# The last ticks of a fused cross-attention and DiT block written out call by call, with the MLP's copies, last normalisations and modulations on VectorE

## The reference

```
x = x + attention(q from ada_ln(x), k and v from ada_ln(ctx)) @ Wp            # layer CROSS0
x = x + gate_a * (attention(modulate(ln(x))) @ W_proj)                        # layer SELF1
x = x + attention(q from ln(x), k and v from ln(ctx)) @ W_cproj               # layer CROSS1
h = modulate(ln(x), shift_m, scale_m)                                         # 16 x 128 x 128
x = x + gate_m * (gelu(h @ W_mlp1 + b_mlp1) @ W_mlp2 + b_mlp2)                # inner width 512
```

## Time and profile before

| what | value |
|---|---|
| median of 3 runs | 291.34 us |
| the profiled execution's own time | 289.38 us |
| its span in the profile | 287.6 us |
| PE busy | 244.8 us, 85% |
| ACT busy | 219.7 us, 76% |
| DVE busy | 217.9 us, 76% |
| POOL busy | 135.8 us, 47% |
| granted PE clock, mean | 0.976 of full speed |

### The profile page before, as it was taken

The page is one execution under the profiler, slowest core; times in us unless marked ns, Lnnn a source line. Parts: engine busy times, 40 slices in busy tenths (PEclk is TensorE's granted clock), DMA queues, the critical chain, the costliest instruction groups (busy, mean ns, idle before and its releaser), DMA issues.

```text
span 287.6 us, 10124 instructions
## 1 busy us (share of the span) xinstructions
PE 244.8 (85%) x3811; PEld 171.0 (59%) x3811; DVE 217.9 (76%) x452; ACT 219.7 (76%) x399; POOL 135.8 (47%) x286
## 2 busy tenths in 40 slices
PE   1836888998898998989999899998998788887995
PEld 1523544766666666665666666676666455554865
DVE  6887886989789797887988899888997776313323
ACT  5327296897978879788798887988879688799940
POOL 8450723836336173363846738466275163420500
PEclk9975899999999999999999999999999999999999
DMA  6085965433446335452433424324244000000112
GB/s 202 10 189 145 254 139 169 134 97 100 128 131 147 101 98 132 128 132 61 109 98 82 114 56 119 98 71 115 60 113 109 10 5 6 3 2 0 36 53 59
DMA packets 34223, 27.44 MB, mean 95 GB/s; under 512 B 4904, under 2 KB 33920, under 8 KB 34176
## 3 DMA queue, kind: packets, MB, share of 16 engines
q1 hardware_dynamic: 32678, 25.54, 34.1%
q10 hardware_dynamic: 1498, 1.26, 1.9%
HBM read 6.46 MB, written 1.06 MB: 26 GB/s over the span
## 4 chain that ended last, share of the span: by engine, by line
PE 39%; ACT 23%; issue 12%; DVE 11%; POOL 9%; DMA 4%; SPq 1%; ACTq 1%; POOLq 0%; DVEq 0%
PE all_ps L469 8%; ACT probs L739 6%; PE all_ps L534 6%; ACT normed L705 6%; PE keyed_ps L520 5%; POOL parts L1117 4%; PE all_ps L576 4%; PE score_ps L495 4%; PE all_ps L565 3%; PE all_ps L557 3%; DVE rest L924 3%; DMA stack_k<-parts 3%; ACT parts L719 3%; DVE normed L909 2%; POOL parts L1115 2%
## 5 line engine op out<-in xcount | busy, mean ns | idle before, releaser
L932 DVE TENSOR_REDUCE neg_max<-score_ps 128x8 f32<-128x1024 f32 x96 | 117.3, 1222 | 18.8 <-PE score_ps L495 17.9
L739 ACT ACTIVATE probs<-keyed_ps 128x1024 f32<-128x1024 f32 x96 | 98.3, 1024 | 18.7 <-PE keyed_ps L520 14.5
L534 PE MATMUL all_ps<-probs,values 128*32 128x128 f32 x1536 | 54.4, 277 | 0.9 <-ACT probs L739 0.5
L534 PEld LDWEIGHTS all_ps<-probs,values 128*32 128x32 f32 x1536 | 37.9, 109 | 17.7 <-issue 8.9
L520 PE MATMUL keyed_ps<-stack_q,stack_k 64*128 64x128 bf16 x768 | 37.8, 217 | 6.0 <-ACT probs L739 5.6
L495 PE MATMUL score_ps<-stack_k,stack_q 62*128 62x128 bf16 x768 | 38.2, 219 | 5.5 <-DMA stack_k<-parts 1.9
L1102 POOL CAST max_parts<-neg_max 128x16 bf16<-128x16 f32 x48 | 9.8, 204 | 64.3 <-DVE neg_max L932 64.3
L495 PEld LDWEIGHTS score_ps<-stack_k,stack_q 62*128 62x128 bf16 x768 | 23.9, 95 | 16.1 <-issue 10.8
L520 PEld LDWEIGHTS keyed_ps<-stack_q,stack_k 64*128 64x128 bf16 x768 | 23.6, 94 | 16.4 <-ACT probs L739 13.8
L1085 POOL TENSOR_TENSOR rstd<-var_eps,minus_half 128x4 f32<-128x4 f32 x24 | 24.4, 1016 | 18.2 <-DVE var_eps L897 18.0
L469 PE MATMUL all_ps<-normed_t,w_qk 128*128 128x512 f32 x48 | 28.8, 694 | 0.0
(11 more groups left out here) (104 smaller groups left out, 402.1 us busy)
## 6 DMA issues: line engine op xcount, KB each, us to landing
stack_q<-parts SPq DMA_DIRECT2D x72, 128.0 KB, 2.5
stack_k<-parts SPq DMA_DIRECT2D x66, 128.0 KB, 2.8
gate<-gate_d SPq DMA_DIRECT2D x16, 128.0 KB, 3.2
stack_q<-max_rows SPq DMA_DIRECT2D x96, 4.0 KB
xs<-in_x_dram SPq DMA_DIRECT2D x4, 256.0 KB, 3.3
cs<-in_ctx_dram SPq DMA_DIRECT2D x4, 256.0 KB, 4.1
out_dram<-xs SPq DMA_DIRECT2D x8, 128.0 KB, 1.8
stack_k<-parts ACTq DMA_DIRECT2D x6, 128.0 KB, 3.6
```

Source lines behind the costliest of these rows:

```text
L534: mm = pe.matmul(ps[QUAD * a:QUAD * (a + 1), c * T:(c + 1) * T], values[:, u // PER % STACKS, u % PER * PAIRS + CP * c + a, 2 * e:2 * e + ...
L739: act.activation(probs[:, n % 3, :], keyed_ps[:, :, :].rearrange("t e n -> t (e n)"), ACT.Exp, scale=float(D) ** -0.5).then_inc(probs_read ...
L932: dve.tensor_reduce(neg_max[:, u % 2, :, CP * c:CP * (c + 1)], score_ps[:, :, :].rearrange("t e (a k) -> t e a k", k=T), AX.X, ALU.max, ne ...
```

## The change

The loops of all engines end at tick 44 (`DRAIN`), and from there each engine has a written list of calls; `DRAIN_USES` repeats PE's list for the ring. On ACT `leave_hidden` is gone for pieces 0 to 11, on DVE it is new; pieces 12 to 15 stay on ACT with their Gelu. Groups 14 and 15 are normalised by DVE's `normalise` and modulated by a new `modulate_mlp` on DVE, where ACT did both; POOL leaves out the two offset instructions for them. `activate_hidden` now waits for one piece at a time. Pieces 0 and 1 still have their ticks 41 and 42. The diff, cut to its core:

```diff
-        LAST = 57
-        UP_AT = (41, 42, 44, 44, 44, 45, 46, 46, 48, 48, 49, 50, 51, 52, 52, 53)
-        DOWN_AT = (49, 50, 51, 51, 53, 54, 55, 56)
-        GELU_AT = (48, 49, 51)
-        ADD_AT = (50, 52, 52, 52, 53, 53, 53, 54)
+        UP_AT = (41, 42)
+        DVE_FROM = 14
+        DRAIN = 44
         ACT_NORMS = (0,)
...
+        DRAIN_USES = [("max", 46), ("proj", 42), ("out", 43), ("up", 2), ("up", 3), ("turn", 43),
...
+        USES = HEAD_USES + [use for tick in range(FIRST, DRAIN) for use in at_tick(tick)] + DRAIN_USES
...
+            move_max(46)
+            move_max(47)
...
+            attend(43, 1)
+            scores(47, 0)
+            keyed_scores(44, 0)
+            turn_max(46)
+            project_out(42)
+            turn_summed(43)
+            keyed_scores(44, 1)
+            scores(47, 1)
+            mlp_up(0, 2)
+            mlp_up(0, 3)
+            turn_attn(43)
+            keyed_scores(45, 0)
+            turn_max(47)
+            mlp_up(1, 0)
+            attend(44, 0)
+            attend(44, 1)
+            project_out(43)
+            turn_summed(44)
+            attend(45, 0)
+            keyed_scores(45, 1)
+            turn_attn(44)
+            mlp_up(1, 1)
+            attend(45, 1)
+            keyed_scores(46, 0)
+            project_out(44)
+            turn_summed(45)
+            keyed_scores(46, 1)
+            turn_attn(45)
+            mlp_up(1, 2)
+            mlp_up(1, 3)
+            attend(46, 0)
+            attend(46, 1)
+            project_out(45)
+            keyed_scores(47, 0)
+            transpose_normed(14, 0)
+            turn_summed(46)
+            keyed_scores(47, 1)
+            attend(47, 0)
+            turn_attn(46)
+            attend(47, 1)
+            project_out(46)
+            turn_summed(47)
+            turn_attn(47)
+            mlp_up(2, 0)
+            mlp_up(2, 1)
+            project_out(47)
+            mlp_up(2, 2)
+            mlp_down(0, 0)
+            mlp_down(0, 1)
+            mlp_up(2, 3)
+            transpose_normed(15, 0)
+            mlp_down(1, 0)
+            mlp_down(1, 1)
+            mlp_up(3, 0)
+            mlp_up(3, 1)
+            mlp_up(3, 2)
+            mlp_up(3, 3)
+            mlp_down(2, 0)
+            mlp_down(2, 1)
+            mlp_down(3, 0)
+            mlp_down(3, 1)
...
             def leave_hidden(n):
-                q, c = n // MLP, n % MLP
+                c = n % MLP
                 act.wait_ge(hidden_ps, n + 1)
-                if q == 2 and c == 0:
-                    act.wait_ge(normed_ready[1], nth(GROUPS - 1, 1) + 1)
-                if q == 3 and c == 0:
+                if c == 0:
                     act.wait_ge(mlp_ps, 2)
-                ins = act.activation(hidden_of(q, c), bank("up", n), ACT.Identity if q < 3 else ACT.Gelu_apprx_tanh,
-                                     bias=bcol[:, R_MLP1 + c:R_MLP1 + c + 1])
-                ins.then_inc(pre_ready if q < 3 else hidden_ready, 1)
-            def activate_hidden(q):
-                act.wait_ge(pre_ready, MLP * q + MLP)
-                for c in range(MLP):
-                    act.activation(hidden_of(q, c), hidden_of(q, c), ACT.Gelu_apprx_tanh).then_inc(hidden_ready, 1)
+                act.activation(hidden_of(3, c), bank("up", n), ACT.Gelu_apprx_tanh,
+                               bias=bcol[:, R_MLP1 + c:R_MLP1 + c + 1]).then_inc(hidden_ready, 1)
+            def activate_hidden(q, c):
+                act.wait_ge(pre_ready, MLP * q + c + 1)
+                act.activation(hidden_of(q, c), hidden_of(q, c), ACT.Gelu_apprx_tanh).then_inc(hidden_ready, 1)
...
+            copy_summed(43)
+            exponentials(44, 0)
+            exponentials(44, 1)
+            exponentials(45, 0)
+            attn_with_bias(43)
+            copy_summed(44)
+            exponentials(45, 1)
+            attn_with_bias(44)
+            copy_summed(45)
+            exponentials(46, 0)
+            exponentials(46, 1)
+            attn_with_bias(45)
+            copy_summed(46)
+            exponentials(47, 0)
+            exponentials(47, 1)
+            attn_with_bias(46)
+            copy_summed(47)
+            activate_hidden(0, 0)
+            activate_hidden(0, 1)
+            attn_with_bias(47)
+            activate_hidden(0, 2)
+            activate_hidden(0, 3)
+            activate_hidden(1, 0)
+            activate_hidden(1, 1)
+            activate_hidden(1, 2)
+            activate_hidden(1, 3)
+            activate_hidden(2, 0)
+            activate_hidden(2, 1)
+            activate_hidden(2, 2)
+            activate_hidden(2, 3)
+            leave_hidden(12)
+            leave_hidden(13)
+            leave_hidden(14)
+            leave_hidden(15)
...
+            def leave_hidden(n):
+                q, c = n // MLP, n % MLP
+                dve.wait_ge(hidden_ps, n + 1)
+                if q == 2 and c == 0:
+                    dve.wait_ge(normed_ready[1], nth(GROUPS - 1, 1) + 1)
+                dve.tensor_scalar(hidden_of(q, c), bank("up", n), bcol[:, R_MLP1 + c:R_MLP1 + c + 1], None,
+                                  ALU.add).then_inc(pre_ready, 1)
+            def modulate_mlp(g):
+                b0, b1 = batches(g)
+                dve.wait_ge(normed_ps[0], g + 1)
+                dve.wait_ge(normed_t_ready[0], g)
+                for b in range(b0, b1):
+                    ins = dve.tensor_scalar(mlp_in[:, b, :], bank("norm", g, 0)[:, (b - b0) * T:(b - b0 + 1) * T],
+                                            mod[:, M_SCALE[LAYERS], b:b + 1], mod[:, M_SHIFT[LAYERS], b:b + 1], ALU.mult, ALU.add)
+                ins.then_inc(normed_t_ready[0], 1)
...
+                for n, at in enumerate(UP_AT):
+                    if at == tick:
+                        leave_hidden(n)
+            copy_max_rows(46)
+            row_max(47, 0)
+            divide(43)
+            row_max(47, 1)
+            add_branch(42)
+            leave_hidden(2)
+            leave_hidden(3)
+            copy_max_rows(47)
+            leave_hidden(4)
+            add_branch(43)
+            norm_stats(14, 0)
+            divide(44)
+            leave_hidden(5)
+            add_branch(44)
+            divide(45)
+            normalise(14, 0)
+            leave_hidden(6)
+            add_branch(45)
+            leave_hidden(7)
+            divide(46)
+            modulate_mlp(14)
+            add_branch(46)
+            divide(47)
+            leave_hidden(8)
+            add_branch(47)
+            norm_stats(15, 0)
+            leave_hidden(9)
+            leave_hidden(10)
+            add_mlp(0)
+            normalise(15, 0)
+            leave_hidden(11)
+            modulate_mlp(15)
+            add_mlp(1)
+            add_mlp(2)
+            add_mlp(3)
+            add_mlp(4)
+            add_mlp(5)
+            add_mlp(6)
+            add_mlp(7)
...
-                if n in ACT_NORMS and g >= 2:
+                if n in ACT_NORMS and 2 <= g < DVE_FROM:
...
+            add_out_bias(43)
+            split_max(47)
+            add_out_bias(44)
+            inverse_root(14, 0)
+            add_out_bias(45)
+            add_out_bias(46)
+            add_out_bias(47)
+            inverse_root(15, 0)
+            add_mlp_bias(2)
+            add_mlp_bias(3)
```

More of the change, by code:

```diff
@@ L589, in _ @@
             scores(0, 1)
-            for tick in range(FIRST, LAST):
+            for tick in range(FIRST, DRAIN):
                 if unit(tick - 1):
@@ L1040, in _ @@
                     normalise(g, 1)
-                for n in range(B // 2):
-                    if ADD_AT[n] == tick:
-                        add_mlp(n)
                 g = front(tick, -10, 1)
```

31 lines of the change are left out of this document (14 added, 17 removed).

## The result

The change makes the kernel about 0.5% slower: 292.87 us against 291.36 us (20 executions each, medians), a ratio of 1.0054 with a 95% interval of 1.0027 to 1.008. A second series gave 1.0023 (0.9973 to 1.0074). The forecast was 291.5 us in a range that ended at 292.4.

The account below looks back on a forecast made before the run. PE was taken as the bound from tick 44 on, so only its idle time could be won: -1.5 us there plus 1.7 us at group 15 gave +0.2 us, hence 291.5 us, range 289.7 to 292.4 us.

Parts of the forecast that it names:

- the hold: At group 15, POOL's SBUF instructions block DVE's add and normalisation; PE waits about 1.7 us before the transpose.
- nothing is added: Behind group 15's transpose, DVE's last copy and modulation fit within 3.6 us of second products, costing 0 us.
- the first part: From tick 44 on, PE's idle time: 2.9 us of waits go, 1.4 us come, a gain of 1.5 us.
- The copy out of PSUM: DVE's 128x512 copy with bias, absent from the trace before, was priced at 0.7 us.
- Fourteen of them: The number of new DVE copies, said to total 10 us on an engine idle for 30 of 45 us.
- S: Start of unit 47's add on DVE, 263.98 before; the normalisation was to end near S + 6.85, PE arriving at S + 5.1.
- B: Rival at group 15: no hold, or one that DVE wins; -1.5 us, 289.8 us, chance 0.27.
- Sum: Whole kernel: -1.5 us of idle time plus 1.7 us at group 15 gives +0.2 us.
- Tells 0.2% from no change: Claim that a measurement of this kernel can resolve a difference of 0.2%, 0.6 us.
- C: Rival from tick 44 on: DVE's copies make PE wait in four places, +1.0 us, 292.5 us, chance 0.15.
- A: The forecast itself: gains and the loss at group 15 cancel, -0.3 to +0.7 us, 291.5 us, chance 0.58.
- the idle time for the transposed result of unit 44: Wait for DVE's division, forecast at about 0.6 us; above 0.9 us at units 44 to 46 would show C.

Follow-up runs that it names:

- bias_early_add1: bias_early with DVE's add_mlp(1) ahead of its last copy and modulation; 54.54 us from first MLP piece to last matmul, ratio 0.9972 to the kernel before.
- bias_early: The change with POOL's quarter 2 bias and quarter 3 product ahead of the last power; 55.09 us from first MLP piece to last matmul, ratio 0.993 to before.
- pieces01_act: The change with MLP pieces 0 and 1 copied by ACT in ticks 41 and 42 as before; 57.09 us from first MLP piece to last matmul.
- move_only: Kernel before with its order, but copies and groups 14 and 15's normalisation and modulation on DVE; 58.36 us from first MLP piece to last matmul, ratio 1.0073.
- after_again: The change itself, run and profiled once more; 56.87 us from first MLP piece to last matmul, ratio 1.0023 to the kernel before.
- best_a: bias_early_add1 with DVE's division of unit 44 ahead of group 14's statistics; ratio 0.9916 to the kernel before, its profiled execution 540 us.

## Why the prediction was wrong

The mechanism was the one forecast, at the place forecast. The step that failed most is the one behind the hold, "nothing is added": a bank is waited for there, 0.40 us. Two more terms were too small, the hold by 0.2 us and the first part by 0.1. With the 0.94 us that the trace shows, the time would be 292.3 us, still inside the range. The other 0.6 us of the 1.5 between the medians was not found in the trace, so that the range was left is partly bad luck.

- *First part, PE's idle time: -1.5 us.* Measured 54.54 - 55.93 = -1.39 us once the hold and the bank are taken out (bias_early_add1). The sum held, its pieces less so. From the first piece to unit 47's transposed result I had -0.5 us, and it was -0.10 (32.48 us before, 32.38 in bias_early). By places, from start to start: ahead of the first scores of unit 47 it gained 0.21, where I had nothing (pieces01_act: it is the two copies). Around units 43 and 44, where the MLP pieces moved, I had -0.06 and it was +0.22; around the transposed result of unit 44 I had +0.34 and it was +0.47: the waits went and came as forecast (0.45 us for the division), but the calls around the moved pieces and between the two halves of a product overlap less than they did. At the second keyed scores of unit 47 I had -0.58 and it was -0.37, since PE waits 0.22 us there for a bank that DVE's copy frees. The other places came within 0.05. Around units 43 to 45 the new order thus cost 0.7 us, where move_only, with the old order, lost nothing. Behind it I had -1.0, and it was -1.3: the projection of unit 47 alone gave 0.69 us (2.58 us from the transposed result to it before, 1.89 after), the part behind the transpose of group 15 0.51.
- *The copy out of PSUM: 0.7 us.* Measured 0.75 us at 250.92, the upper row; two in a row 1.40. "Fourteen of them" was a slip: DVE makes twelve, some 8 us and not 10. The sum does not use it.
- *The hold: +1.7 us.* Measured +1.93 us (41.72 - 39.79). Held were the SBUF add, to 0.3 us after POOL's end, and two of the four normalising instructions, to 0.1 us after; the four took 3.14 us in all. PE came at S + 5.1 as forecast (S is 264.27 here), and the four ended at S + 7.0, not 6.85. The Trainium skill, in SBUF — State Buffer, section "SBUF: two separate sides", states that whoever starts first has the shared ports for the whole instruction, and that a DVE instruction with two SBUF inputs is blocked only by a GpSimd instruction that reads SBUF. The products, adds and memsets here agree with that, down to the add that a memset does not hold. The power on 128x4 does not: it reads SBUF, lasts 1.02 us and held neither kind. B, that the pauses between POOL's instructions would let DVE through, fell: DVE got one instruction into each pause.
- *"Behind it ... nothing is added".* I asked whether the last quarter's input would be ready, and it was; I did not ask for the bank of the second product in between, which waits for `add_mlp(1)` behind the copy and the modulation. It cost 15.15 - 14.75 = 0.40 us in the change.
- *Sum:* -1.39 + 1.93 + 0.40 = +0.94 us, the stretch's difference, where I had +0.2. The rest of the 1.5 us between the medians is not placed; it is within the scatter, since after_again shows 0.45 us between medians with the same stretch. "Tells 0.2% from no change" was too hopeful: the first series has an interval of 0.5%, the second of 1%.
- *C, DVE becomes what PE waits for*, was given 0.15 with copies as its cause. The stretch came out 0.24 us above A's upper end of +0.7, and that is a piece of C: both banks wait for DVE's queue. The copies had a small part in it (0.22 us at unit 46's `summed`, and one of the two calls ahead of `add_mlp(1)`); the idle time for the transposed result of unit 44 is 0.45 us, not above 0.9.

## What to carry to other kernels

Before handing an SBUF-to-SBUF step to VectorE, look at what GpSimd does in the same microseconds: here the products, adds and memsets of GpSimd each held a VectorE instruction that reads and writes SBUF until they ended. So put GpSimd's long ones where VectorE reads PSUM or idles or where nobody waits for what is held, or cut them short; here that turned a loss of 0.9 us into a gain of 0.8. When work is moved onto an engine, follow every result that this engine frees (banks too), not only those that it makes. Try the move in the old order before writing a new one, and compare them part by part. And where executions scatter by more than the effect, compare a stretch of the trace that begins at the first changed instruction: it repeated within 0.02 us where the times spread by 8.

## What was not expected of the hardware

- A single DVE normalising instruction beside a POOL product of 128x512 took up to 1.41 us instead of 0.34, beside a memset 0.59; a DVE add with two SBUF inputs was held by a product or an add (up to 1.26 instead of 0.42 us) and not by a memset. A power of 1.02 us on 128x4 held neither.
- The scatter of 8 us between executions lies wholly ahead of the last fifth: the first piece of the MLP began between 228.15 and 236.85 us, while the 55 us behind it repeated (best_a's execution of 540 us apart). What causes it was not examined.
